# Ten semaphore increments per pair of batches in TensorE's program, in a gated cross-attention and expert kernel

## The chip, the cores and the metric

The kernel runs on one core of a Trainium2 chip. The time is that of the device for one execution, in microseconds (us); three executions of the kernel before took 1228.09, 1228.75 and 1229.5 us.

## The reference

Inputs: x is 32 batches of 56 tokens with 256 features, ctx is 32 batches of 1500 context rows with 256 features, all in float32. What is computed:

```
q = layernorm(x) @ Wq.T + bq          # 16 heads of 16
k = ctx @ Wk.T + bk ; v = ctx @ Wv.T + bv
p = softmax(mask(clip(q.k / 4)))      # over 1500 context rows, per head
delta = rs * ((p @ v) @ Wo.T + bo)
x1 = x + tanh(g_xattn) * (layernorm(delta) * gamma + beta)
y  = layernorm(x1); logits = y @ w_router; weights of the best 2 of 8 experts
out = x1 + tanh(g_ffn) * sum over experts of weight * (relu(y @ w_fc)^2 @ w_proj)
```

Nearly all of the work is the projection of the 48,000 context rows to keys and values, the scores, and the weighted sum of values (here called PV).

## The kernel before, in words

The 32 batches are worked off in 16 pairs (NP). A pair's context is cut in 6 groups (PG) of 500 rows, and a group in 4 chunks (GC) of 125 rows, so a pair has 24 chunks. Two operands that must keep float32 accuracy are each split in a high and a low part, and a product is made of three matmuls.

TensorE's program is written out in full: `for i in range(1, NP): pair(i)` is a Python loop, and no loop instruction is in the program. For each of a pair's 6 groups q it does, in this order:

- PV of the 4 chunks of the group before (`pv`, line 497): 128 short matmuls with 56 columns, each with a weight load of 17 columns.
- small work of neighbouring pairs (`beside_pv`): at q = 3 the router, the query projection (line 514) and the output projection (line 521), at q = 5 two transposes (lines 506 and 527).
- the scores of the 4 chunks (`scores`, line 482), interleaved with four parts of the key and value projections of the next group (`kv_part`, lines 456 and 459). These matmuls have 224 to 500 columns.

ScalarE takes the exponential of the scores (line 687), VectorE clips it (line 992), and TensorE's PV waits for the clipped tile. SyncE loads the context, one group per transfer. After the last pair comes the expert stage (`fc` and `proj`, which call `mm3` at lines 399 to 401), 7 tiles of 256 tokens by 8 experts.

TensorE waits on semaphores with `wait_ge`. Some of these waits are carried by a weight load, others are instructions of their own (EVENT_SEMAPHORE in the profile, under the name PEldq, the queue of TensorE). Each matmul is two instructions, a LDWEIGHTS (PEld) and a MATMUL (PE). Instructions come to the engine by DMA, on queues of the kind "instruction".

Of the kernel before, what the change touches and what calls it, by code (L numbers as in the profile page):

```python
# [27 lines left out]
PG = 2 * NG  # L28
# [10 lines left out]
UN = PC // 2  # L39
NW = 2 * NE  # L40
NB = 4

CST = (P, NE, HS, KD, KD)
# [9 lines left out]
def gated_cross_attention_moe(nc, a, x1_dram, sums_dram, inv_dram, out):  # L54
# [5 lines left out]
    with ExitStack() as ctx:  # L60
        def sem(name):
            return ctx.enter_context(nc.semaphore(name))

        def sb(name, shape, dt=fp32, scope=ctx):
            return scope.enter_context(nc.sbuf_tensor(name, shape, dt))

        def plain(ap):
            return ap.bitcast(fp32)

        def wait(eng, s, value):  # L70

            if not isinstance(value, int) or value > 0:
                eng.wait_ge(s, value)
# [89 lines left out]
        h_sq = sb("h_sq", [P, 2, KD, FT], scope=ffn)  # L163
        h_hi = sb("h_hi", [P, NB, KD, FT], fp32r, scope=ffn)
        h_lo = sb("h_lo", [P, NB, KD, FT], fp32r, scope=ffn)
        ffn.close()
# [89 lines left out]
        acc_done = sem("acc_done")  # L256
        out_done = sem("out_done")
        dve_seq = sem("dve_seq")

        block = ctx.enter_context(nc.Block())  # L260

# [74 lines left out]
        def _(pool):  # L336
# [40 lines left out]
            def h_low(f):  # L377

                for e in range(NE):
                    u = f * NE + e  # L380
                    at = step(f, e)
                    pool.wait_ge(hhi_done, u + 1)
                    pool.tensor_tensor(h_lo[:, e % NB, :, :], h_sq[:, e % 2, :, :], plain(h_hi[:, e % NB, :, :]),  # L383
                                       ALU.subtract).then_inc(hlo_done, 1)
# [11 lines left out]
        def _(pe):  # L396
            def mm3(ps, w_h, w_l, m_h, m_l, first, last):

                pe.matmul(ps, w_h, m_h, start=first, stop=False)  # L399
                pe.matmul(ps, w_h, m_l, start=False, stop=False)  # L400
                return pe.matmul(ps, w_l, m_h, start=False, stop=last)  # L401
# [26 lines left out]
            def kv_terms(s, k):  # L428

                return ((wk_hi, c_hi[:, s, k, :]), (wk_hi, c_lo[:, s, k, :]), (wk_lo, c_hi[:, s, k, :])), \  # L430
                       ((c_hi[:, s, k, :], wv_hi), (c_hi[:, s, k, :], wv_lo), (c_lo[:, s, k, :], wv_hi))

            def kv_part(n, half, s, part, freed=()):

                if part == 0:
                    if half == 0:
                        pe.wait_ge(ctx_split, KD * (n + 1))
                    for side in freed:
                        wait(pe, *side)
                    wait(pe, k_lo, KD * (n - 1) + half + 1)  # L440
                    wait(pe, v_evac, 2 * n + half)
                else:
                    pe.wait_ge(kpart_done, 2 * (n - 1) + half + 1)
                    pe.wait_ge(vpart_done, 2 * (n - 1) + half + 1)
                k_rows = slice(part * HW, (part + 1) * HW)
                v_rows = slice((1 - part) * HW, (2 - part) * HW)
                ws = slice(half * P, (half + 1) * P)
                for k in range(KD):
                    k_terms, v_terms = kv_terms(s, k)
                    for t in range(3):  # L450
                        begin, end = part == 0 and k == 0 and t == 0, part == 1 and k == KD - 1 and t == 2
                        w, c_m = k_terms[t]
                        c_s, w_m = v_terms[t]
                        for j in range(2):
                            cs = slice((2 * half + j) * TC, (2 * half + j + 1) * TC)
                            v_last = pe.matmul(v_ps[0:TC, j * D:(j + 1) * D], c_s[v_rows, cs], w_m[v_rows, k, :],  # L456
                                               start=begin and j == 0, stop=end, skip_group_check=True)
                            if j == 0:
                                k_last = pe.matmul(k_ps[:, half, 0:TG], w[k_rows, k, ws], c_m[k_rows, :],  # L459
                                                   start=begin, stop=end)  # L460
                if part == 0:
                    k_last.then_inc(kpart_done, 1)
                    v_last.then_inc(vpart_done, 1)
                else:
                    k_last.then_inc(kproj_done, 1)
                    v_last.then_inc(vproj_done, 1)
# [19 lines left out]
            def pv(i, c):  # L486

                n = i * PC + c
                if c % NC == 0:
                    wait(pe, o_evac, 2 * i + c // NC)  # L490
                if c % 2 == 0:
                    pe.wait_ge(v_evac, i * UN + c // 2 + 1)
                pe.wait_ge(clip_done, n + 1)
                for h in range(NH):
                    col, q = divmod(h, ST)
                    at = (h // HS % 2 * KD + h // (2 * HS)) * HS + h % HS
                    last = pe.matmul(o_ps[q * 32:q * 32 + VW, col * S:(col + 1) * S], vst[0:TC, c // GC % 2, c % GC, h, :],  # L497
                                     prob[0:TC, c % PB, at * S:(at + 1) * S], start=(c % NC == 0 and col == 0),
                                     stop=(c % NC == NC - 1), skip_group_check=True)
                last.then_inc(pv_done, 1)  # L500
# [38 lines left out]
            def pair(i):  # L539
                first, late, final = i == 0, i >= NP - 2, i == NP - 1  # L540
                freed = {3: [], 5: []}
                if not first:
                    freed[3].append((dlt_evac, i))
                    freed[5].append((ylo_done, i + 1))
                if not final:
                    freed[3].append((qT_done, i + 2))
                if not late:
                    freed[5].append((xT_done, i + 3))
                if first:
                    freed[1] = [(xT_done, 2)]  # L550
                for q in range(PG):
                    n = i * PG + q + 1
                    c, slot = GC * q, (q + 1) % 2
                    more = not (final and q == PG - 1)
                    if first and q == 1:
                        pe.wait_ge(o_clear, 1)
                    if not (first and q == 0):
                        for d in range(GC, 0, -1):
                            pv(*((i, c - d) if q > 0 else (i - 1, PC - d)))
                    beside_pv(i, q, first, late, final)  # L560
                    if more:
                        kv_part(n, 0, slot, 0)
                    scores(i, c)
                    if more:
                        kv_part(n, 0, slot, 1)
                    if first and q == 0:
                        pe.wait_ge(v_evac, 2)
                    scores(i, c + 1)
                    scores(i, c + 2)
                    if more:  # L570
                        kv_part(n, 1, slot, 0, freed.get(q, ()))
                    scores(i, c + 3)
                    if more:
                        kv_part(n, 1, slot, 1)

            def beside_pv(i, q, first, late, final):

                if q in (3, 5) or (first and q == 1):
                    pe.wait_ge(k_lo, KD * (i * PG + q + 1))
                if first and q == 1:  # L580
                    x_transpose(1)
                if q == 3:
                    for t in range(routed(i - 1), routed(i)):
                        pe.wait_ge(ylo_done, i)
                        pe.wait_ge(wr_split, 18)
                        router(0, t)
                if q == 3 and not final:
                    q_proj(i + 1)
                if q == 3 and not first:
                    out_proj(i - 1)  # L590
                if q == 5 and not late:
                    x_transpose(i + 2)
                if q == 5 and not first:
                    y_transpose(i - 1)
# [28 lines left out]
            def proj(f, e):  # L623
# [4 lines left out]
                for t in range(2):  # L628
                    ts = slice(t * P, (t + 1) * P)
                    for k in range(KD):  # L630
                        last = mm3(sc_ps[:, 2 + e % 2, t * D:(t + 1) * D], h_hi[:, e % NB, k, ts], h_lo[:, e % NB, k, ts],
                                   we_hi[:, 2 * e + 1, k, :], we_lo[:, 2 * e + 1, k, :], k == 0, k == KD - 1)
# [34 lines left out]
        def _(act):  # L667
# [117 lines left out]
            def hidden(f, first=False):  # L785
                for e in range(NE):
# [7 lines left out]
                    act.wait_ge(sq_done, u + 1)  # L794
                    if not (first and e < NB):
                        act.wait_ge(y2_done, u - NB + 1)
                    act.activation(h_hi[:, e % NB, :, :], h_sq[:, e % 2, :, :], ACT.Copy).then_inc(hhi_done, 1)  # L797
# [427 lines left out]
```

## Time and profile before

| what | value |
|---|---|
| profiled execution | 1228.58 us |
| its span, first to last instruction | 1226.4 us |
| median of three executions | 1228.75 us |
| TensorE matmul busy | 1192.0 us, 97% |
| TensorE weight load busy | 1149.7 us, 94% |
| VectorE busy | 855.7 us, 70% |
| ScalarE busy | 684.9 us, 56% |
| mean granted clock of TensorE | 0.996 of full speed |

The span is what the core took from its first to its last instruction. Busy time is the union of an engine's instructions; those of TensorE overlap, so its busy share says only that it has hardly a gap. Gaps are found in the views of waits, where "issue" means that the engine waited for nothing that the profile shows.

### The profile page before, as it was taken

To read this page: it belongs to the slowest core of one execution; us is meant where nothing else is said; L and a number is where in the kernel's file an instruction comes from. 1 tells how busy PE (TensorE), PEld (TensorE's weight loads), DVE (VectorE), ACT (ScalarE), POOL (GpSimd) and SP (SyncE) were. 2 spreads that over 40 slices of the span, in tenths; PEclk is the share of its full clock that TensorE was granted. 3 is DMA by queue.
4 is the path that set the end of the run, shared out by engine and by line. 5 is a ranking of instruction groups with operands and counts; after the bars stand their busy time and mean duration, and the time that the engine had idled before them with its cause. 6 is when DMAs were issued, how large, how long until landed. Compare 5 with 4: busy or idle time off the path is not lost. (4 is left out here: it accounts for less than half of the span.)

```text
span 1226.4 us, 56179 instructions
## 1 busy us (share of the span) xinstructions
PE 1192.0 (97%) x25428; PEld 1149.7 (94%) x25428; DVE 855.7 (70%) x1715; ACT 684.9 (56%) x838; POOL 144.1 (12%) x142
## 2 busy tenths in 40 slices
PE   6899999999999999999999999999999999999998
PEld 6899999999999999999999999999999999899998
DVE  5567777767777777676767777677767676788555
ACT  3466565656565656565655665565656555534443
POOL 0000000000000000000000000000000010244443
PEclk9899999999999999999999999999999999999999
DMA  4122121222221212121222211222212120210000
GB/s 144 57 65 68 53 71 65 67 69 67 68 67 40 91 44 81 55 74 46 69 67 70 67 61 60 67 67 69 65 39 78 55 71 29 66 28 10 18 10 18
DMA packets 36858, 72.87 MB, mean 59 GB/s; under 512 B 11221, under 2 KB 20754, under 8 KB 36626
## 3 DMA queue, kind: packets, MB, share of 16 engines
q1 hardware_dynamic: 27746, 58.57, 15.8%
q10 hardware_dynamic: 8880, 10.75, 2.6%
q8 instruction: 201, 3.29, 1.1%
q14 instruction: 31, 0.25, 0.1%
HBM read 64.48 MB, written 3.90 MB: 56 GB/s over the span
## 5 line engine op out<-in xcount | busy, mean ns | idle before, releaser
L687 ACT ACTIVATE prob<-sc_ps,m_bias 125x896 f32<-125x896 f32 x384 | 377.3, 1009 | 336.8 <-PE sc_ps L482 336.4
L456 PE MATMUL v_ps<-wv_hi,c_hi 64*125 64x256 f32 x1520 | 312.2, 285 | 2.7 <-DVE c_lo L846 2.6
L459 PE MATMUL k_ps<-c_hi,wk_hi 64*128 64x500 f32 x760 | 306.2, 403 | 0.0
L456 PE MATMUL v_ps<-wv_lo,c_hi 64*125 64x256 f32 x1520 | 302.3, 278 | 0.9 <-issue 0.9
L456 PE MATMUL v_ps<-wv_hi,c_lo 64*125 64x256 f32 x1520 | 301.6, 278 | 0.0
L459 PE MATMUL k_ps<-c_lo,wk_hi 64*128 64x500 f32 x760 | 293.5, 386 | 0.5 <-issue 0.5
L459 PE MATMUL k_ps<-c_hi,wk_lo 64*128 64x500 f32 x760 | 293.0, 385 | 0.0
L855 DVE TENSOR_TENSOR vst<-v_ps,rowv 125x512 f32<-125x512 f32 x191 | 131.4, 688 | 212.8 <-PE v_ps L456 212.8
L992 DVE TENSOR_SCALAR prob<-prob 125x896 f32<-125x896 f32 x384 | 235.6, 620 | 36.1 <-ACT prob L687 36.0
L456 PEld LDWEIGHTS v_ps<-wv_hi,c_hi 64*125 64x125 f32 x1520 | 226.7, 184 | 16.3 <-issue 5.8
L482 PE MATMUL sc_ps<-q_lo,kh 64*125 64x224 f32 x1536 | 233.2, 270 | 0.6 <-issue 0.5
L482 PE MATMUL sc_ps<-q_hi,kl 64*125 64x224 f32 x1536 | 232.8, 269 | 0.0
L482 PE MATMUL sc_ps<-q_hi,kh 64*125 64x224 f32 x1536 | 231.4, 267 | 1.2 <-issue 0.8
L456 PEld LDWEIGHTS v_ps<-wv_lo,c_hi 64*125 64x125 f32 x1520 | 229.1, 183 | 1.5 <-issue 1.5
L456 PEld LDWEIGHTS v_ps<-wv_hi,c_lo 64*125 64x125 f32 x1520 | 229.8, 183 | 0.0
L482 PEld LDWEIGHTS sc_ps<-q_hi,kh 64*125 64x125 f32 x1536 | 198.4, 185 | 2.0 <-issue 1.0
L497 PE MATMUL o_ps<-prob,vst 125*17 125x56 f32 x12288 | 176.1, 214 | 10.6 <-DVE prob L992 5.3
L497 PEld LDWEIGHTS o_ps<-prob,vst 125*17 125x17 f32 x12288 | 157.1, 98 | 28.3 <-issue 19.1
L482 PEld LDWEIGHTS sc_ps<-q_hi,kl 64*125 64x125 f32 x1536 | 170.1, 186 | 0.6 <-issue 0.6
L482 PEld LDWEIGHTS sc_ps<-q_lo,kh 64*125 64x125 f32 x1536 | 169.4, 185 | 0.3 <-issue 0.3
L673 ACT ACTIVATE kh<-k_ps,cst 128x500 fp32r<-128x500 f32 x192 | 130.6, 680 | 67.7 <-PE k_ps L459 67.0
L459 PEld LDWEIGHTS k_ps<-c_lo,wk_hi 64*128 64x128 f32 x760 | 142.0, 187 | 0.7 <-issue 0.7
(133 smaller groups left out, 1956.3 us busy)
## 6 DMA issues: line engine op xcount, KB each, us to landing
raw<-in_ctxT SPq DMA_DIRECT2D x96, 500.0 KB, 3.6
w_raw<-in_we ACTq DMA_DIRECT2D x16, 256.0 KB, 3.9
rec<-inv_scratch SPq DMA_DIRECT2D x64, 56.0 KB, 2.0
xq<-in_x ACTq DMA_DIRECT2D x16, 112.0 KB, 2.9
xr<-in_x ACTq DMA_DIRECT2D x16, 112.0 KB, 3.7
x_scratch<-x ACTq DMA_DIRECT2D x16, 112.0 KB, 3.7
out_y<-acc SPq DMA_DIRECT2D x7, 256.0 KB, 2.0
acc<-x_scratch SPq DMA_DIRECT2D x1, 1280.0 KB, 6.1
```

The costliest lines, as they stand in the source:

```text
L456: v_last = pe.matmul(v_ps[0:TC, j * D:(j + 1) * D], c_s[v_rows, cs], w_m[v_rows, k, :], start=begin and j == 0, stop=end, skip_group_check ...
L459: k_last = pe.matmul(k_ps[:, half, 0:TG], w[k_rows, k, ws], c_m[k_rows, :], start=begin, stop=end)
L482: last = pe.matmul(sc_ps[0:TC, 2 * (c % 2) + r, m * HS * S:(m + 1) * HS * S], k[rows, g % 2, m, cs], q[rows, b, m, :, :], start=term == 0, ...
L497: last = pe.matmul(o_ps[q * 32:q * 32 + VW, col * S:(col + 1) * S], vst[0:TC, c // GC % 2, c % GC, h, :], prob[0:TC, c % PB, at * S:(at + ...
L673: act.activation(kh[:, s, m, :], k_ps[:, m, 0:TG], ACT.Identity, bias=bk[:, m:m + 1]).then_inc(k_hi, 1)
L687: act.activation(prob[0:TC, c % PB, :].rearrange("p (c n) -> p c n", c=2), sc_ps[0:TC, 2 * (c % 2):2 * (c % 2) + 2, 0:NH * S // 2], ACT.Ex ...
L855: dve.tensor_tensor(vst[0:TC, s, 2 * half:2 * half + 2, :, 0:HD], v_bank[0:TC, :].rearrange("p (j h d) -> p j h d", j=2, h=NH), bv[0:TC, : ...
L992: dve.tensor_scalar(p, p, EXP_LO, EXP_HI, ALU.max, ALU.min).then_inc(clip_done, 1)
```

## The change

A semaphore `pe_filler` is made that nobody waits on, and TensorE increments it ten times after its work on group q = 4 of each pair, ahead of PV at q = 5.

```
+FILL = 10
...
+        pe_filler = sem("pe_filler")
...
             def pair(i):
...
                 for q in range(PG):
...
                     scores(i, c + 3)
                     if more:
                         kv_part(n, 1, slot, 1)
+                    if q == PG - 2:
+                        whole_lines()
+
+            def whole_lines():
+
+                for _ in range(FILL):
+                    pe.sem_inc(pe_filler, 1)
```

## Rows read from the trace of the kernel before

**Rows 1.** The page: busy time by engine, and the instruction queues (packets, MB, share)
```profile
span 1226.4 us, 56179 instructions
PE 1192.0 (97%) x25428; PEld 1149.7 (94%) x25428; DVE 855.7 (70%) x1715; ACT 684.9 (56%) x838; POOL 144.1 (12%) x142
q8 instruction: 201, 3.29, 1.1%
```

**Rows 2.** Windows from one pair's first PV to the next: length, busy (count) by engine
```profile
core 0: us, PE busy (x) PEld busy (x) DVE busy (x) ACT busy (x) POOL busy (x), PEclk, DMA share, GB/s
99.84:163.27 63.43, 63.14 (x1507) 60.93 (x1505) 46.12 (x93) 38.43 (x45) 4.34 (x5) 1.00 0.22 66
...
290.57:354.44 63.87, 63.57 (x1511) 61.37 (x1509) 46.44 (x95) 38.45 (x45) 4.33 (x5) 1.00 0.21 66
354.44:418.32 63.88, 63.58 (x1511) 61.37 (x1509) 46.45 (x95) 38.45 (x45) 4.34 (x5) 1.00 0.21 66
418.32:482.37 64.05, 63.75 (x1510) 61.48 (x1508) 46.44 (x95) 38.44 (x45) 4.33 (x5) 1.00 0.22 66
482.37:547.50 65.13, 64.08 (x1510) 61.62 (x1508) 46.45 (x95) 38.46 (x45) 4.34 (x5) 1.00 0.22 64
547.50:613.46 65.96, 64.66 (x1511) 61.93 (x1509) 46.54 (x95) 38.45 (x45) 4.34 (x5) 1.00 0.21 64
613.46:679.83 66.37, 64.90 (x1510) 61.98 (x1508) 46.53 (x95) 38.43 (x45) 4.33 (x5) 1.00 0.21 63
679.83:745.30 65.47, 64.21 (x1506) 61.35 (x1505) 46.21 (x93) 38.45 (x45) 4.34 (x5) 1.00 0.21 64
745.30:811.10 65.80, 64.34 (x1511) 61.70 (x1509) 46.44 (x95) 38.47 (x45) 4.34 (x5) 1.00 0.20 64
811.10:875.64 64.54, 64.27 (x1511) 61.57 (x1509) 46.35 (x95) 38.38 (x45) 4.33 (x5) 1.00 0.21 65
875.64:940.82 65.18, 63.98 (x1509) 61.34 (x1509) 46.45 (x95) 38.41 (x45) 4.34 (x5) 1.00 0.21 64
940.82:1005.96 65.14, 63.64 (x1508) 61.30 (x1507) 45.81 (x90) 38.07 (x44) 3.80 (x4) 1.00 0.22 63
```

**Rows 3.** Waits of the weight loads, window 482 to 1057: us, times, longest
```profile
PEld o_ps L497 <- issue: 11.8, 40, 0.7
PEld v_ps L456 <- issue: 5.0, 14, 1.2
```

**Rows 4.** Timeline of weight loads, PV at q = 1, pairs 1, 8, 9 and 10
```profile
99.84 1.61 PEld L497 LDWEIGHTS o_ps<-prob,vst 125*17 125x17 f32 x128
...
547.50 1.40 PEld L497 LDWEIGHTS o_ps<-prob,vst 125*17 125x17 f32 x109 [0.15 <-issue]
549.29 0.31 PEld L497 LDWEIGHTS o_ps<-prob,vst 125*17 125x17 f32 x19 [0.39 <-issue]
...
613.46 1.49 PEld L497 LDWEIGHTS o_ps<-prob,vst 125*17 125x17 f32 x114 [0.15 <-issue]
615.60 0.23 PEld L497 LDWEIGHTS o_ps<-prob,vst 125*17 125x17 f32 x14 [0.66 <-issue]
...
679.83 1.50 PEld L497 LDWEIGHTS o_ps<-prob,vst 125*17 125x17 f32 x119
681.53 0.16 PEld L497 LDWEIGHTS o_ps<-prob,vst 125*17 125x17 f32 x9 [0.20 <-issue]
```

**Rows 5.** DMA of one pair, window 482.37 to 547.50: packets of TensorE's instruction queue
```profile
q8 instruction: 12, 0.20, 1.2%
```

**Rows 6.** Waits of the weight loads in the last pair, window 1005.96 to 1057
```profile
PEld sc_ps L482 <- issue: 0.9, 2, 0.6
```

**Rows 7.** A stall after PV, timeline of weight loads
```profile
889.72 0.18 PEld L456 LDWEIGHTS v_ps<-wv_lo,c_hi 64*125 64x125 f32 x1 [1.19 <-issue]
```

**Rows 8.** The wait ahead of PV at q = 5, window 331.5 to 332, and PV's weight loads
```profile
L493 PEldq EVENT_SEMAPHORE  x1: 51/51/51, 331.7 to 331.7; - x1
...
333.26 1.61 PEld L497 LDWEIGHTS o_ps<-prob,vst 125*17 125x17 f32 x128
```

**Rows 9.** All semaphore instructions of line 493 on TensorE, durations in ns
```profile
L493 PEldq EVENT_SEMAPHORE  x192: 51/51/51, 28.7 to 1058.7; - x192
```

## The prediction

> **What bounds the kernel now.** I read the page first. TensorE's matmuls are busy for 1192.0 of 1226.4 us, and no other engine passes 70% [rows 1], so an instruction added to TensorE's program can only be paid for there, and so can a gap that goes. The question is then whether TensorE has gaps that depend on where its instructions lie. The same page says how they arrive: 201 packets with 3.29 MB on the instruction queue, 16.4 KB a packet [rows 1]. TensorE has 2 x 25,428 instructions of matmuls and, by the code, some 790 semaphore waits; 51,650 over 201 packets is 257 for one packet. I take a packet ("line") as 256 instructions, or 64 bytes each, and a pair draws 12 of them [rows 5]. 12 lines would be 3072 instructions, the number in the title of the change; the pair has 3062 now.
>
> Next I cut the attention stage into windows, each from a pair's PV at q = 1 to the next pair's. The reader should see that the same work takes 63.43 us in pair 1 (no router yet), 63.87 and 63.88 us in pairs 4 and 5, and then more, up to 66.37 us in pair 9, with the same counts of matmuls, the same busy time of VectorE and ScalarE, and a granted clock of 1.00 in all [rows 2]. So neither the work nor the clock nor another engine makes pair 9 longer. The waits name no releaser: PV stands still 40 times for 11.8 us with nothing the profile shows to wait for ("issue"), and the value projection 14 times for 5.0 us, in the second half [rows 3]. Some 0.15 us of each of those is the usual turn from one kind of tile to the other.
>
> The timeline shows where in PV it stops. In pair 8 it stops after 109 of the 128 weight loads, in pair 9 after 114, in pair 10 after 119, and in pair 1 not at all [rows 4]. It moves by 5 weight loads, which is 10 instructions, per pair: exactly 3072 less 3062. A stop whose place in the work drifts by 10 instructions while its place in the program repeats every 3072 is a line boundary. PV consumes instructions fastest: 128 weight loads and 128 matmuls in 1.61 us [rows 4], that is 6.3 ns each, where the rest of a pair takes 63.88 - 6 x 1.61 = 54.2 us for some 1,526 instructions, 36 ns each. A line that is almost all PV is used up in 1.6 to 3 us, and the next line isn't there yet. One that is half PV takes 128 x 6.3 ns + 128 x 36 ns = 5.4 us, and nothing stops. A group is some 503 to 530 instructions, about two lines, so when the phase is bad, it is bad for all six groups of a pair at once.
>
> **The change part by part.** *The phase.* The ten increments stand once in each pair, so a pair becomes 12 whole lines, and the phase stops drifting. Where it stops is what counts. By pair 8's PV at q = 1, eight sets have gone by: 80 instructions are 40 weight loads, so the boundary in PV falls after load 109 - 40 = 69. In pair 9 it is 114 - 45 = 69, in pair 10 119 - 50 = 69. After pair 10, which has no router tile (its window has x1506 instead of x1511 [rows 2]) and so 8 instructions less, it is 73. At q = 2 to 5 it varies by the side work to some 65 to 85. The kernel before had the boundary at 69 only in its first two pairs, and at 89 (109 less 20) in pair 4, and both ran at full speed [rows 2]. Stops begin, by the windows, in pair 6 with 0.17 us. So positions 66 to some 100 are shown free, and the pinned phase lies in them with 15 or more loads to spare. I let every stop at a line boundary in the attention stage go.
>
> *What that is worth.* Against 63.88 us the windows of pairs 6 to 9 are over by 0.17, 1.25, 2.08 and 2.49 us; pair 10, without its router, is measured against pair 1's 63.43 and is over by 2.04; pairs 11 to 14 are over by 1.92, 0.66, 1.30 and 1.26 [rows 2]. Sum: 13.17 us. In the last pair two stops in the scores make up 0.9 us [rows 6], and by the starts around them perhaps 1.1; I take 1.0. The total is 14.2 us. What is late next? Nothing that isn't late in pairs 4 and 5 as well, because the pairs are alike, and those run at 63.88 us with VectorE at 46.45 us [rows 2]. The expert stage has no PV, uses a line in far longer, and I change nothing there.
>
> *The increments.* 16 x 10 of them. The trace of before has no increment that is an instruction of its own on TensorE; the nearest is the wait, recorded at 51 ns, all 192 alike [rows 9]. Behind them is queued PV at q = 5, for which VectorE's copy of PV's sum and the next pair wait. The cover is the queue of issued work: the wait that stands at that very place is handled at 331.7 us and its PV begins at 333.26, 1.6 us later [rows 8]. So TensorE still has 1.6 us of projection matmuls before it when its queue comes to the increments. Ten at 51 ns are 0.51 us, within 1.6: cost nothing. From below I exclude a gain by themselves, since nobody waits on this semaphore. From above, with no cover at all, it is 160 x 51 ns = 8.2 us. I take 0, since the row for the cover is taken at the same place.
>
> The page "Runtime: NRT & Kernel Launch" of the Trainium skill, in "Instruction fetch mechanics", has instructions come in blocks of 256, and says that "the cost of crossing a 16 KiB boundary is one DMA tail-bump, mostly hidden". By that rule no alignment matters, and the sum would be 0. The block size agrees with the rows; "mostly hidden" holds for pairs 1 to 5, and not for a PV that stops for up to 0.7 us.
>
> *Sum.* The profiled execution took 1228.58 us, 0.17 under the median of 1228.75. 1228.58 - 14.2 + 0 = 1214.4 us.
>
> **The rivals.**
> 1. *The increments are paid for in part*, either because one takes longer than a wait, or because PV's instructions come late to a queue that was held up. For it: no row shows ten sequencer instructions in a row ahead of PV. Against: 1.6 us of cover [rows 8], and single waits inside PV leave it at 1.61 us. Up to 8.2 us are given back: 1222.6; halfway, 1218.5.
> 2. *The pinned phase is a bad one*, so that every pair is like pair 9. It ends slower. It would need the boundary after load 105 or later of the 128, where I find 65 to 85, for instance if the program's start moved by a third of a line, or if one of the two lines in a group is short of time in a way that pairs 1 to 5 hid. Price: 15 pairs by 2.49 us [rows 2] are 37 us on top of 1214.4, 1251 us; it becomes a loss from 14.2 / 15 = 0.95 us a pair.
> 3. *An increment drains the engine or takes long.* With 1.6 us of cover it eats the whole gain when ten cost 1.6 + 14.2 / 16 = 2.5 us, 250 ns each, five times the row of the wait. The time would be 1228.6 at that point, and slower beyond.
> 4. *The change doesn't do what it says*: the increments are folded into fewer instructions, so that a pair stays short of 3072. With all folded into one, the drift is 9 instead of 10 and the stops shift a pair: 1227 or so. Also in this class: the stops aren't due to the lines (a DMA that collides with them, for instance), and nothing changes: 1228.6. The drift of 5 loads speaks against it, and so does a stop of 1.19 us in the projection just behind PV [rows 7], where PV had filled the line before it.
>
> **How the numbers follow.** Forecast as worked out 0.78; rival 1 0.12; rival 2 0.03; rival 3 0.03; rival 4 0.04. Within 0.2% (2.5 us) of 1228.75 cannot be told from no change. Faster: 0.78 + 0.12 and a share of 4, 0.92. Same: 0.04. Slower: 0.04. The range goes down to 1212.5, as the free pairs may hide small stops of their own and the sum has pieces of 0.1 us that I can't separate, and up to 1221.5, to take in most of rival 1.
>
> **What would show it.** Right: all windows of pairs 3 to 13 at 63.9 us (63.4 without router), "issue" waits of PV down to the 0.15 us turns, PV always x128 unbroken, PV at q = 5 beginning as long after the group's start as in pair 4, and still 12 packets a pair. Wrong: a gap of its own before every PV at q = 5 means that the increments cost; pairs that are all longer by the same amount with PV broken at one fixed load mean rival 2; breaks that still wander mean rival 4.

## The result, and the profile after

The changed kernel took 1213.39 us (median of four executions, 1212.23 to 1213.87), the kernel before 1228.42 (1227.92 to 1229.5). The ratio is 0.987, with a 95% interval of 0.9858 to 0.9883: 15.0 us less. The profiled execution took 1213.63 us, its span 1211.8. The forecast was 1214.4, with a range of 1212.5 to 1221.5.

The pairs' windows, cut as in [rows 2] from a pair's first PV to the next pair's, for pairs 1, 4, 6 and 8 to 14:

```profile
core 0: us, PE busy (x) PEld busy (x) DVE busy (x) ACT busy (x) POOL busy (x), PEclk, DMA share, GB/s
99.69:163.11 63.42, 63.19 (x1506) 60.95 (x1504) 46.11 (x93) 38.45 (x45) 4.33 (x5) 1.00 0.22 66
...
290.43:354.32 63.89, 63.66 (x1510) 61.40 (x1509) 46.44 (x95) 38.45 (x45) 4.33 (x5) 1.00 0.21 66
...
418.19:482.07 63.88, 63.65 (x1510) 61.41 (x1508) 46.44 (x95) 38.45 (x45) 4.33 (x5) 1.00 0.22 66
...
545.94:609.81 63.87, 63.64 (x1511) 61.40 (x1509) 46.45 (x95) 38.42 (x45) 4.33 (x5) 1.00 0.22 66
609.81:673.67 63.86, 63.63 (x1510) 61.39 (x1508) 46.44 (x95) 38.43 (x45) 4.33 (x5) 1.00 0.22 66
673.67:737.11 63.44, 63.21 (x1507) 60.96 (x1505) 46.12 (x93) 38.43 (x45) 4.33 (x5) 1.00 0.21 66
737.11:800.97 63.86, 63.63 (x1510) 61.39 (x1508) 46.45 (x95) 38.43 (x45) 4.33 (x5) 1.00 0.21 66
800.97:864.86 63.89, 63.66 (x1511) 61.41 (x1509) 46.45 (x95) 38.44 (x45) 4.33 (x5) 1.00 0.22 66
864.86:928.74 63.88, 63.65 (x1511) 61.41 (x1509) 46.44 (x95) 38.44 (x45) 4.32 (x5) 1.00 0.22 66
928.74:992.68 63.94, 63.29 (x1509) 61.20 (x1507) 45.88 (x90) 38.19 (x44) 3.79 (x4) 1.00 0.22 64
```

Every pair from 3 to 14 now takes what pairs 4 and 5 took before, within 0.1 us, but for pair 10, which has no router and takes the 63.4 us of pair 1. Pair 9 went from 66.37 to 63.86 us. The counts of instructions and the busy times of VectorE and ScalarE are those of [rows 2] within 0.1 us or so, so no engine has less work; TensorE stopped waiting. TensorE's queue still takes 12 packets of instructions in a pair. The waits of the weight loads, window 482 to 1043, which answer to [rows 3] (us, times, longest):

```profile
PEld o_ps L499 <- issue: 5.1, 30, 0.2
PEld v_ps L458 <- issue: 3.1, 9, 0.3
```

PV's waits without a releaser fell from 11.8 us in 40 to 5.1 us in 30, and the longest is 0.2 us, the turn between two kinds of tile. PV at q = 1 of pair 9, which stopped after load 114 in [rows 4], goes through (timeline of weight loads):

```profile
609.80 1.61 PEld L499 LDWEIGHTS o_ps<-prob,vst 125*17 125x17 f32 x128
```

The increments are the new thing in the trace. The ten of pair 4, window 331.5 to 333.1, and the PV behind them:

```profile
L583 PEldq EVENT_SEMAPHORE  x10: 51/51/51, 331.5 to 333.0; - x10
...
333.21 1.64 PEld L499 LDWEIGHTS o_ps<-prob,vst 125*17 125x17 f32 x128 [0.22 <-issue]
```

Each is recorded at 51 ns, as the wait of [rows 9] is, but the ten are spread over 331.5 to 333.0 us. Read in narrow windows, the first starts at 331.54 and the last at 332.98: eight of the nine steps are 0.15 us and one is 0.24. So ten take about 1.5 us of the queue and not 0.51, nearly all of its lead of 1.6 us [rows 8]. The windows of q = 4 and q = 5 of pair 4, from PV to PV, before and after, show what came of it. Before:

```profile
323.20:333.27 10.07, 10.07 (x251) 9.84 (x249) 8.18 (x19) 6.19 (x7) 0.88 (x1) 1.00 0.17 54
333.27:344.38 11.11, 10.81 (x255) 10.24 (x253) 7.68 (x15) 6.93 (x9) 0.00 (x0) 1.00 0.30 94
```

After:

```profile
323.08:333.24 10.16, 10.13 (x250) 9.85 (x249) 8.27 (x19) 6.20 (x7) 0.88 (x1) 1.00 0.16 54
333.24:344.26 11.02, 10.82 (x253) 10.25 (x253) 7.59 (x15) 6.92 (x9) 0.00 (x0) 1.00 0.30 95
```

PV at q = 5 comes 0.1 us later, with a gap of 0.22 us ahead of it that stands there in the other pairs too, and the group behind it is 0.1 us shorter. The time is taken back at the transposes of q = 5, which wait for VectorE anyway (timeline, before and after):

```profile
335.33 0.20 PEld L506 LDWEIGHTS k_ps<-cst,xn 112*128 112x128 f32 x2 [0.46 <-DVE kl L840]
```

```profile
335.20 0.20 PEld L508 LDWEIGHTS k_ps<-cst,xn 112*128 112x128 f32 x2 [0.35 <-DVE kl L849]
```

### The profile page after: what moved, and what is told of

The parts are those of the page before. It is cut to its first block, busy times and chain, and to the rows that moved or that the text cites. A ratio compares the mean times of both kernels' runs of the same rounds, so it can differ in the third digit from the quotient of the medians.

```text
span 1211.8 us, 56339 instructions
## 1 busy us (share of the span) xinstructions
PE 1186.1 (98%) x25428; PEld 1147.2 (95%) x25428; DVE 855.5 (71%) x1715; ACT 685.0 (57%) x838; POOL 143.9 (12%) x142
## 4 chain that ended last, share of the span: by engine, by line
PE 86%; DVE 10%; issue 2%; DMA 1%; ACT 1%; POOL 1%; POOLq 0%; SPq 0%; DVEq 0%; ACTq 0%
PE v_ps L458 22%; PE k_ps L461 21%; PE sc_ps L484 18%; PE o_ps L499 11%; PE sc_ps L401 3%; PE sc_ps L403 3%; PE sc_ps L402 3%; DVE prob L1001 2%; DVE vst L864 2%; DVE kl L849 2%; PE k_ps L516 1%; PE k_ps L523 1%; DVE c_lo L855 1%; DVE q_hi L901 1%; PE k_ps L508 1%
## 5 line engine op out<-in xcount | busy, mean ns | idle before, releaser
L484 PE MATMUL sc_ps<-q_lo,kh 64*125 64x224 f32 x1536 | 230.1, 270 | 0.0
L484 PE MATMUL sc_ps<-q_hi,kl 64*125 64x224 f32 x1536 | 229.8, 269 | 0.0
L484 PE MATMUL sc_ps<-q_hi,kh 64*125 64x224 f32 x1536 | 228.7, 268 | 0.5 <-ACT prob L696 0.5
L499 PE MATMUL o_ps<-prob,vst 125*17 125x56 f32 x12288 | 170.9, 213 | 5.7 <-DVE prob L1001 5.3
L499 PEld LDWEIGHTS o_ps<-prob,vst 125*17 125x17 f32 x12288 | 155.6, 98 | 20.7 <-issue 14.6
L484 PEld LDWEIGHTS sc_ps<-q_hi,kl 64*125 64x125 f32 x1536 | 166.0, 186 | 0.0
L484 PEld LDWEIGHTS sc_ps<-q_lo,kh 64*125 64x125 f32 x1536 | 165.1, 185 | 0.0
```

The source lines that it names most:

```text
L484: last = pe.matmul(sc_ps[0:TC, 2 * (c % 2) + r, m * HS * S:(m + 1) * HS * S], k[rows, g % 2, m, cs], q[rows, b, m, :, :], start=term == 0, ...
```

## The experiments

All kernels below start from the changed one. "Load" is the number of PV's 128 weight loads ahead of the line boundary at q = 1. Each ratio is to the kernel before. A time is the median of its executions; the windows are from the profiled one, whose time can differ from the median by up to 4.5 us (experiment 3).

```
             pe.wait_ge(cst_in, 16)
+            for _ in range(41):
+                pe.matmul(sc_ps[0:16, 1, 0:8], ident[:, 0:16], ident[:, 0:8], start=True, stop=True)
             x_transpose(0, first_side)
```

> The changed kernel, with 41 tiny matmuls (164 instructions) once at TensorE's start, in the 7 us in which it waits for its first input. A pair stays 3072 instructions, but the line boundary in PV at q = 1 moves from load 69 to load 115, where pair 9 of the kernel before had it. Theory (the position of the line boundary decides): each of 15 pairs takes some 66.3 us in place of 63.8, and the time is 1213.4 + 15 x 2.49 = 1250 us, slower than the kernel before. Rival (the increments help by themselves, or the length of 3072 does, whatever the position): 1213 to 1214 us.

Measured: 1259.64 us, ratio to before 1.0235 (1.0211 to 1.0258). Windows of pairs 3, 6 and 12, and PV at q = 1 of pair 9:

```profile
237.98:304.68 66.70, 64.72 (x1510) 61.81 (x1508) 46.53 (x95) 38.45 (x45) 4.32 (x5) 1.00 0.20 63
...
438.60:504.22 65.62, 64.78 (x1511) 61.83 (x1509) 46.53 (x95) 38.42 (x45) 4.33 (x5) 1.00 0.22 64
...
836.06:903.68 67.62, 64.61 (x1510) 61.90 (x1508) 46.54 (x95) 38.45 (x45) 4.32 (x5) 1.00 0.20 62
```

```profile
636.53 1.50 PEld L499 LDWEIGHTS o_ps<-prob,vst 125*17 125x17 f32 x116
638.68 0.22 PEld L499 LDWEIGHTS o_ps<-prob,vst 125*17 125x17 f32 x12 [0.66 <-issue]
```

The same ten increments in each pair, the same 3072 instructions, and 46 us slower than the changed kernel. The 14 windows of pairs 1 to 14 add up to 930.50 us against 892.99, so 2.7 us a pair. That makes the position the cause, and neither the increments nor the length. About 10 us more than expected came partly from single long stops in PV, one of 3.54 us that ends at 84.3 and one of 2.47 us that ends at 1082.3. The instruction packets say something about both. In the 2.47 us stop 127 of PV's 128 loads went by ahead of it, so the whole line was PV, and its packet took 1.7 us where others take 0.9 to 1.5. In the other the packet started only at 81.66 us, 2.25 us behind the start of that PV, where in pairs 3 and 9 it starts some 0.55 us ahead of it; from 79 to 82 us the windows have the DMA engines 0.83 to 1.04 busy with other transfers. That transfers of data can hold up a line fits this, but no run varied them.

**2. One shift, no increments** (shift_once).

```
-                    if q == PG - 2:
-                        whole_lines()
...
+            for _ in range(24):
+                pe.matmul(sc_ps[0:16, 1, 0:8], ident[:, 0:16], ident[:, 0:8], start=True, stop=True)
```

> No increments in the pairs; instead 24 tiny matmuls (96 instructions) once at TensorE's start. A pair is 3062 instructions again and the boundary drifts by 5 loads a pair, but 96 instructions later. Theory (position): the stretch in which the kernel before stopped (pairs 6 to 15) is moved out behind the last pair but for q = 2 and 3 of pair 15 (some 0.5 us), while pairs 0 and 1 come into the position of pairs 11 to 13 of the kernel before (0.7 to 1.9 us each): 1214 to 1217 us. Rival (the increments in each pair are needed): 1228 us.

Measured: 1228.19 us, ratio 0.9986 (0.9973 to 0.9999). By its total this is the rival's number. The windows say otherwise (pairs 1, 2, 3, 4, 5, 6, 9 and 10, from an execution of 1225.98 us):

```profile
99.08:166.52 67.44, 64.26 (x1507) 61.38 (x1505) 46.17 (x93) 38.47 (x45) 4.33 (x5) 1.00 0.20 62
166.52:233.92 67.40, 64.35 (x1507) 61.39 (x1505) 46.10 (x93) 38.37 (x45) 4.34 (x5) 1.00 0.21 62
233.92:299.23 65.31, 64.25 (x1511) 61.70 (x1509) 46.45 (x95) 38.47 (x45) 4.33 (x5) 1.00 0.21 64
299.23:364.63 65.40, 64.09 (x1511) 61.49 (x1509) 46.45 (x95) 38.37 (x45) 4.34 (x5) 1.00 0.20 64
364.63:428.78 64.15, 63.87 (x1511) 61.49 (x1509) 46.45 (x95) 38.45 (x45) 4.34 (x5) 1.00 0.21 65
428.78:492.67 63.89, 63.59 (x1511) 61.39 (x1509) 46.43 (x95) 38.41 (x45) 4.33 (x5) 1.00 0.23 66
...
620.55:684.43 63.88, 63.58 (x1511) 61.38 (x1509) 46.45 (x95) 38.42 (x45) 4.33 (x5) 1.00 0.22 66
684.43:747.86 63.43, 63.13 (x1507) 60.94 (x1505) 46.12 (x93) 38.41 (x45) 4.34 (x5) 1.00 0.22 66
```

Pairs 6 to 10 run at full speed with no increment in them, so increments aren't needed for that. What I had wrong was the price of the other end: pairs 1 to 5 are over by 4.0, 4.0, 1.4, 1.5 and 0.3 us. There the boundary comes early in PV, load 18 to 46, and the line is used up in PV and a little of the slow part. A boundary early in PV costs more than one late in it, and the drift of 5 loads or more a pair over 15 pairs is wider than the free stretch between the two.

**3. The early boundary, pinned** (phase_200). As experiment 1, with `range(20)`.

> The changed kernel with 20 tiny matmuls (80 instructions) once at TensorE's start: pairs of 3072 instructions, with the line boundary after load 29 of PV at q = 1, where the run with 24 tiny matmuls and no increments had it in its pair 2 (window 67.40 us against 63.43). Theory (a line that begins in PV and ends in the slow part behind it is short of time too): 4 us in each of 15 pairs, 1265 to 1275 us. Rival (only a line that is nearly all PV is too fast, and this one has 86 instructions at 36 ns in it): 1214 to 1220 us.

Measured: 1277.11 us, ratio 1.0375 (1.0345 to 1.0406). Window of pair 9, and one of its stops, in the scores behind PV:

```profile
655.56:724.05 68.49, 65.08 (x1511) 61.93 (x1509) 46.44 (x95) 38.51 (x45) 4.33 (x5) 1.00 0.20 61
```

```profile
660.10 0.18 PEld L484 LDWEIGHTS sc_ps<-q_hi,kl 64*125 64x125 f32 x1 [0.74 <-issue]
```

The 14 windows sum to 955.21 us, 4.4 us a pair over the changed kernel. The lever is large: two kernels that differ in 20 tiny matmuls at the start are 64 us apart.

**4. Half as many increments** (fill_5). `FILL = 5`.

> Five increments a pair instead of ten, so a pair is 3067 instructions and drifts by 5. Theory (position alone): PV's boundary reaches the place of the kernel before's pairs 6 to 9 only in pairs 11 to 15, 0.5 to 2.5 us each, some 6.5 us in all: 1219 to 1221 us. Rival (whole lines are what counts, any drift costs): 1228 us. Rival (half of the increments gives half of the gain): 1221 us as well, but then spread over all pairs; the pair windows tell: 63.9 us up to pair 10.

Measured: 1219.78 us, ratio 0.993 (0.9913 to 0.9947). Pairs 9 and 11 to 14:

```profile
607.19:671.06 63.87, 63.58 (x1511) 61.38 (x1509) 46.42 (x95) 38.41 (x45) 4.33 (x5) 1.00 0.21 66
...
734.48:798.53 64.05, 63.76 (x1511) 61.47 (x1509) 46.41 (x95) 38.41 (x45) 4.33 (x5) 1.00 0.20 65
798.53:863.36 64.83, 64.02 (x1510) 61.51 (x1508) 46.42 (x95) 38.40 (x45) 4.33 (x5) 1.00 0.20 65
863.36:928.96 65.60, 64.44 (x1511) 61.77 (x1509) 46.42 (x95) 38.44 (x45) 4.33 (x5) 1.00 0.21 64
928.96:995.78 66.82, 64.47 (x1509) 61.69 (x1507) 45.92 (x90) 38.18 (x44) 3.78 (x4) 1.00 0.21 61
```

Pairs run at full speed up to pair 10 with 3067 instructions each. Then the windows grow in the order of [rows 2], five pairs later. Whole lines are one way to stay where it is free, and no condition for it.

**5. The increments without cover** (no_cover).

```
+                    if q == 2:
+                        whole_lines()
                     beside_pv(i, q, first, late, final)
...
-                    if q == PG - 2:
-                        whole_lines()
```

> The same ten increments a pair, moved from behind the projection of q = 4 to behind PV of q = 2, where TensorE's queue is only some 0.15 us ahead of the engine. In the changed kernel's trace they follow each other every 151 ns. Theory (one costs 151 ns of the queue, and only the queue's lead of 1.6 us hides ten): each pair grows by 1.51 - 0.15 = 1.36 us, 16 pairs by 22 us, 1235 us, slower than the kernel before. Rival (one costs the 51 ns of its record): 0.36 us a pair, 1219 us. Rival (free, the sequencer is never the limit): 1213.5 us.

Measured: 1235.02 us, ratio 1.0041 (1.0029 to 1.0052). The stop behind PV of q = 2 in pair 4, and the increments there:

```profile
303.19 1.61 PEld L499 LDWEIGHTS o_ps<-prob,vst 125*17 125x17 f32 x128 [0.15 <-issue]
306.19 0.18 PEld L458 LDWEIGHTS v_ps<-wv_hi,c_hi 64*125 64x125 f32 x1 [1.39 <-issue]
```

```profile
L583 PEldq EVENT_SEMAPHORE  x10: 51/51/51, 304.6 to 306.0; - x10
```

The ten starts lie 151 ns apart, nine steps in 1.37 us. The pairs take 65.2 us, 1.3 more than in the changed kernel, and the whole is 21.6 us slower (18.8 between the profiled executions), as 151 ns each had it (22), and not as 51 ns had it (5.8). The same ten instructions cost next to nothing or some 20 us by where they stand, and here they eat more than the whole gain.

**6. Five and five** (split_5_5). `FILL = 5`, and the call under `if q in (1, 4)`.

> Five increments behind the projection of q = 1 and five behind that of q = 4, so that a pair is still 3072 instructions and each set asks 0.76 us of a lead of 1.6. PV at q = 5 should begin 0.10 us earlier after the group's start than in the changed kernel. Theory (the 0.10 us were paid back by a wait for VectorE at q = 5 anyway): the pair stays at 63.8 us, and the time is 1213.3 us, within 0.2 of the changed kernel. Rival (the 0.10 us a pair are paid in full): 1211.8 us.

Measured: 1213.47 us, ratio 0.987 (0.9854 to 0.9887). q = 4 and q = 5 of pair 4:

```profile
320.54:330.61 10.07, 10.07 (x251) 9.83 (x249) 8.20 (x19) 6.19 (x7) 0.88 (x1) 1.00 0.17 54
330.61:341.72 11.11, 10.81 (x255) 10.24 (x253) 7.68 (x15) 6.92 (x9) 0.00 (x0) 1.00 0.29 94
```

PV at q = 5 is on time again and the group behind it takes its 11.11 us again, so the pair is no shorter: 63.87 us, against 63.89 in the changed kernel.

**7. Matmuls in their place** (mm_filler).

```
-                for _ in range(FILL):
+                for _ in range(FILL // 4):
+                    pe.matmul(o_ps[0:16, 480:488], ident[:, 0:16], ident[:, 0:8], start=False, stop=False,
+                              skip_group_check=True)
+                for _ in range(FILL % 4):
                     pe.sem_inc(pe_filler, 1)
```

> Two tiny matmuls (8 instructions) and two increments in place of ten increments, at the same point. Theory: the phase is the same, and the queue is held up for 0.3 us in place of 1.5, so PV at q = 5 begins 0.10 us earlier than in the changed kernel, which the wait for VectorE behind it takes back: 1213.4 us, within 0.3 of the changed kernel. Rival (the semaphore instructions have a part in it): another time, 1220 or more.

Measured: 1213.18 us, ratio 0.9872 (0.9856 to 0.9889). Two matmuls (eight instructions) and two increments do as well as ten increments. From PV to PV, q = 4 took 10.13 us in pair 4 (323.79 to 333.92), so PV was 0.03 us earlier than in the changed kernel rather than 0.10. The fillers' four weight loads now stand just ahead of it, which would explain this, but no run shows it.

**8. How fast lines come, first try** (line_floor). As experiment 1, with `range(768)`: 12 lines.

> 768 tiny matmuls (3072 instructions, 12 whole lines) once at TensorE's start, in front of the changed kernel, to see how fast lines can come at all. Theory (a line is ready only some 3.5 to 5 us after its turn comes, whatever the engine could do): 12 lines take 42 to 60 us, the kernel 35 to 53 us more than 1213. Rival (a line takes as long as its packet, 1 us, and the stops are something else): the 12 lines run at PV's rate of 1.6 us, 19 us, and the kernel takes some 12 us more.

One execution took 1256.63 us (span 1254.8). A weight load and its matmul in this form take 27 ns, 3.49 us for the 128 of a line, so the engine's own time hid most of what was to be seen: all but two of the stops behind its lines are 0.24 us. The total fits the theory for the wrong reason.

**9. The same in PV's form** (line_floor_4).

```
-            for _ in range(768):
-                pe.matmul(sc_ps[0:16, 1, 0:8], ident[:, 0:16], ident[:, 0:8], start=True, stop=True)
+            for j in range(768):
+                pe.matmul(sc_ps[j % 4 * 32:j % 4 * 32 + 16, 1, 0:8], ident[:, 0:16], ident[:, 0:8], start=True, stop=True)
```

> As the run before with 768 tiny matmuls at the start, but their outputs go round the four groups of 32 columns of the array, as PV's do. In the run before a matmul took 27 ns, so that 256 instructions took 3.49 us of the engine itself, and only 0.24 us of a stop followed most lines: that left open how fast lines can come. In PV's form 256 instructions ask for 1.6 us. Theory (there is a shortest time per line, some 3.3 to 3.7 us): the 12 lines again take 40 to 44 us, with stops of 1.7 to 2.1 us each, and the kernel about 1255 us. Rival (lines come as fast as they are used once the queue is ahead, and the 0.24 us are a fixed price of a boundary): 12 x 1.85 = 22 us, and the kernel 1233 us.

One execution took 1255.9 us (span 1254.0). The timeline of its weight loads at the start:

```profile
4.97 1.95 PEld L607 LDWEIGHTS sc_ps<-cst 128*16 128x16 f32 x224 [4.97 <-DMA cst<-in_cst]
12.10 1.15 PEld L607 LDWEIGHTS sc_ps<-cst 128*16 128x16 f32 x128 [5.18 <-issue]
15.83 1.15 PEld L607 LDWEIGHTS sc_ps<-cst 128*16 128x16 f32 x128 [2.58 <-issue]
19.56 1.15 PEld L607 LDWEIGHTS sc_ps<-cst 128*16 128x16 f32 x128 [2.58 <-issue]
23.01 1.15 PEld L607 LDWEIGHTS sc_ps<-cst 128*16 128x16 f32 x128 [2.31 <-issue]
```

This is a line seen bare: 128 weight loads (256 instructions) go through in 1.15 us, then nothing for 2.3 to 2.6 us, and then the next 128. A line comes every 3.45 or 3.73 us, and in experiment 8, where the engine needs 3.49 us for one, every 3.5 to 4.0. The packet itself isn't the limit: ten of 16 KB take 1.7% of 16 DMA engines in 40 us, 1.1 us each.

```profile
q8 instruction: 10, 0.16, 1.7%
```

The starts of these packets, read in narrow windows, show where the time goes. For the lines begun at 12.10, 15.83 and 19.56 us they are 13.20, 16.96 and 20.67. Over all full lines from there on, a packet starts 1.0 to 1.4 us after the first load of a line, and the next line runs 2.3 to 2.6 us after that. In experiment 8 it is 1.0 to 1.6 us after the first load, though the engine takes three times as long for a line. From this I infer that the following line is asked for when a line is begun, and not earlier. The first stop, 5.18 us, is another matter: its line was begun at about 5.8 us and the packet started only at 9.57, while the windows from 5.8 to 10.6 us have the DMA engines 0.95 to 1.17 busy (in a short window the view can give more than 1). The 3.45 to 3.73 us therefore hold for DMA engines that are nearly idle; what other transfers add to a line no run shows.

## Where the prediction was right and where it was wrong, step by step

*Lines of 256 instructions, and a stop at their boundary.* Right. Experiment 9 shows the 256 directly. Experiments 1 and 3 show that position alone moves the time by 46 and by 64 us with the same work in the pairs.

*Why PV stops.* Right in kind. A line that is nearly all PV is used up in 1.6 to 3 us, and experiment 9 has no line faster than one in 3.45 us. The exact edge is open. Lines whose two boundaries are 3.3 us apart in the engine's time were free on one side (boundary behind load 104, pair 7 of the kernel before) and stopped on the other (pair 9 of experiment 3, from load 29 to the scores). The lead of the queue differs between the two, 1.6 us in the projections [rows 8] and 0.2 in PV (in experiment 5 the first increment is handled at 304.6 and PV's loads end at 304.8), which has the right sign to matter. So has other traffic: in the second case the packet started at 657.64, 1.7 us after load 29 instead of 1.1, in a stretch in which the DMA engines were 0.65 to 1.09 busy. Both are only argued. They may also be why stops at one and the same load differ, 0.18 us in pair 3 and 0.66 in pair 9 of experiment 1.

*The pinned position is free.* Right: no PV of the changed kernel was broken. The count missed that pairs 1 and 2 have no router either. In experiment 1 the stops at q = 1 stand after load 108, 112 and 116 in pairs 1, 2 and 3, so in the changed kernel the boundary is at about 61, 65 and then 69, and not at 69 throughout. By the load at q = 1, full speed was measured from 51 (pair 6 of experiment 2) to 94 (pair 5 of the kernel before), with 0.3 us a pair over at 46 and 0.2 over at 99. Rival 2 was drawn too narrowly. I let a bad position begin only at load 105, and there is a second one below 50 that costs more, 4 us a pair and not 2.49. The margin was therefore some 10 to 15 loads downward, and by the windows of experiment 2 a start shifted by 40 instructions would have lost part of the gain in the first pairs (an estimate).

*The sum.* From the first PV to the last, the kernel before took 1057.06 - 30.34 = 1026.72 us and the changed one 1042.66 - 30.12 = 1012.54: 14.18 us, against 14.2 forecast. Pairs 1 to 14 gave 13.13 of it (forecast 13.17) and the last pair 1.12 (1.0), and pair 0 took 0.07 longer. The medians differ by 15.03 and the profiled executions by 14.95. The 0.8 us over lie outside the pairs: 0.22 in the start, 0.20 behind the last PV, 0.35 outside the span; I don't put these down to the change.

*The increments.* This is the step that failed, though the total did not show it: the term of 0.51 us for ten was mis-sized by three. I priced one at 51 ns by the record of the nearest row [rows 9]; it is 151 ns from one to the next. Ten fill 1.5 us of a cover of 1.6, and PV was late by 0.1 us a pair. The prediction's own sign of rival 1, a gap ahead of every PV at q = 5, is in the trace (0.22 us), but not its price. The total stayed because that lateness ran into a wait of 0.46 us for VectorE (experiment 6). This was luck: the prediction did not count on that wait, and of the cover 0.1 us was left, where its own sum leaves 1.1. With no cover I had bounded the cost at 8.2 us; experiment 5 measured 21.6, outside that bound.

*The page on instruction fetch.* "Runtime: NRT & Kernel Launch" of the Trainium skill calls the crossing of a block "mostly hidden" ("Instruction fetch mechanics"). Here it is hidden in pairs 4 and 5 of the kernel before and in the changed kernel, and bare where a line is used up too soon: up to 2.58 us per line in experiment 9 with the DMA engines nearly idle, and 14.2 us in all in the kernel before.

## What to carry to other kernels

Where a wait on TensorE has no releaser and returns at the same place of the work, moving by a constant number of instructions per iteration, count the instructions between stops: a multiple of 256 points to the instruction lines. Then keep each boundary out of the stretches where instructions are short, by padding, by a shift, or by the order of the work, and check both sides of the free stretch. Filler belongs behind slow matmuls, where the queue is ahead, and its price is the distance between two of them and not the length of one record.

## What the runs showed that I had not expected

- A semaphore increment that is an instruction of its own on TensorE takes 151 ns of its queue, three times its recorded 51 ns. Behind PV ten of them stopped the engine for 1.39 us.
- A line boundary early in the fast stretch costs more than a late one: 4.4 us a pair against 2.7.
- A run of short instructions on TensorE comes at 256 per 3.45 to 3.73 us, 13.5 to 14.6 ns each on average, with the engine needing 4.5 ns (1.15 us for 256).
- The following line seems to be asked for only when a line is begun: its packet starts 1.0 to 1.6 us after the first load, whether the engine needs 1.15 or 3.49 us for a line (experiments 8 and 9). Where the DMA engines were busy with data the packet started later, and the two longest stops at a line boundary, 5.18 and 3.54 us, stand there.
